# Wide attention of a fused decoder: the maxima turned and placed in halves of eight heads, exponentials 13 steps behind the maxima

## The chip, the cores and the metric

The kernel runs on one core of a Trainium2 chip. A core has five engines that this text speaks of: TensorE (PE, whose weight loads the profile lists as PEld), VectorE (DVE), ScalarE (ACT), GpSimd (POOL) and SyncE (SP), which here only issues DMAs. Each works through its own list of instructions in order and waits on semaphores for the others. The metric is the time of one execution on the device in microseconds; lower is better.

## The reference

Twelve residual steps over x of shape (4, 256, 128), four sequences ("batches" b = 0 to 3 below) of 256 tokens. The change lies in the stage that does three of them together: the quantised feedforward of the third layer, and the attention and the cross attention of the fourth.

```python
x = x + _L2_ffn_ref(_layernorm(x), ...)     # two 1.58-bit linear layers, 128 -> 512 -> 128, with layernorm, gelu
x = x + _L3_attn_ref(_layernorm(x), ...)    # the wide attention: 16 heads of 64
x = x + _L3_xattn_ref(_layernorm(x), ...)   # per token, 16 x 16 products of heads

def _L3_attn_ref(x, Wq, bq, Wk, bk, Wv, bv, Wo, bo):
    q, k, v = ...                                # (batch, 16 heads, 256, 64) each
    pattern = jnp.einsum('bhid,bhjd->bhij', k, q) / jnp.sqrt(64)
    prob = jax.nn.softmax(pattern, axis=-2)      # over the keys, for each query
    out = jnp.einsum('bhis,bhid->bhsd', prob, v)
    return concat(out) @ Wo + bo
```

## The kernel before, in words

The stage is `feedforward_attentions`. It is written as a row of steps, from -26 on. Every engine walks through the same steps in order; a semaphore, not a step, is what makes it wait. There are 64 units of the wide attention (4 batches of 16 heads). Step s does, among other things:

- PE `first(s)` (L2133, L2134): the scores of unit s, queries on the partitions, into one of two PSUM banks. The contraction is over 64 rows, and the head's parity decides which half of the array's rows it uses (`r = 64 * (h % 2)`).
- DVE `maxima(s)` (L2392): the largest score of each query. After the last head of a batch four small operations (L2398 to L2404) split the 32 columns of maxima into three bf16 parts.
- PE `second(s - WIDE_LAG)` (L2146, L2147): the scores again, keys on the partitions, minus the maxima, which come in as a product of ones with `MTR`. It also contracts over 64 rows, of the half that its own head's parity gives. ACT (L2249) takes the exponential.
- PE `weighted(s - WIDE_LAG - 1)` (L2163): probabilities times values, over all 128 rows, and every second step DVE `normalise` (L2410, L2412).

The maxima have to get from the partitions to the rows that `second` reads. That is the chain M: PE turns them (job "M", L2094), ACT copies them out (L2217), and SP's queue places them in `MTR` with six DMAs (L2492).

Beside the units runs a plan of jobs, each with a step of its own, at most two to a step (`place` takes the next free step when one is full). A job is some matmuls of PE into one of two banks and a copy out by ACT or DVE. Kinds: f1 to f4 the feedforward, T and xT transposes, q, k and v the projections of the wide attention (L2085, L2089), M the turned maxima, t and o its output projection, x... the cross attention. Pieces such as "gelu" or "products" are work of ACT, DVE and POOL at a given step; the cross attention of a batch is a chain of POOL products (L2456, L2467), DVE sums and an ACT exponential. PE's order inside a step is: jobs, `first`, `second`, `weighted`. ACT's is: copies of jobs, gelu (L2239), the exponential of the cross attention, then the exponential of the unit.

The rule of the plan for batch b before: M at step 16b+18, v from 16b+15, the output projection (t, o) from 16b+40. The feedforward of batch 2 begins at step 1, that of batch 3 at step 16. With `WIDE_LAG` 21, steps 0 to 20 have `first` without `second`, steps 21 to 63 have both, and steps 64 to 84 have `second` without `first`.

Of the kernel before, what the change touches and what calls it, by code (L numbers as in the profile page):

```python
# [9 lines left out]
BF16 = mybir.dt.bfloat16  # L10
I32 = mybir.dt.int32
ALU = mybir.AluOpType
ACT = mybir.ActivationFunctionType
AX_X = mybir.AxisListType.X
# [442 lines left out]
WIDE_LAG = 21  # L457
# [1464 lines left out]
def feedforward_attentions(c):  # L1922
# [9 lines left out]
    MX = s(2 * 32).rearrange("p (r c h) -> p r c h", r=2, c=2)  # L1932
    MR = s(32).rearrange("p (c h) -> p c h", c=2)
    MP = s(2 * 96, BF16).rearrange("p (r c m) -> p r c m", r=2, c=2)
    MT = s(256, BF16)[0:48, :]
# [48 lines left out]
    for b in range(B):  # L1984
        place(16 * b + 18, "M", b, 0)
        for i in range(6):
            place(16 * b + 40 + i + i // 3, ("t", "t", "o")[i % 3], b, i)
# [3 lines left out]
    for b in range(B):  # L1991
# [18 lines left out]
        for i in range(4):  # L2010
            place(16 * b + 15 + i, "v", b, i)
# [16 lines left out]
    assert all(job_at["k", b, i] <= 16 * b + 4 * i and job_at["v", b, 3] < 16 * b + 22 for b in range(B) for i in range(4))  # L2028
# [16 lines left out]
    def tensor(pe, own):  # L2045
# [3 lines left out]
        def run_job(i, kind, b, m):  # L2049
# [41 lines left out]
            elif kind == "M":  # L2091
                pe.wait_ge(max_parts, b + 1)
                for qc in range(2):
                    last = nc.tensor.transpose(out[0:48, 64 * qc:64 * qc + 64].bitcast(BF16), MP[:, b % 2, qc, :], c.identb)  # L2094
# [41 lines left out]
        def second(i):  # L2136
            b, h = i // HEADS, i % HEADS
            if h == 0:
                pe.wait_ge(max_placed, 16 * 6 * (b + 1))
# [27 lines left out]
        for step in range(FROM, TO):  # L2167
            for job in [(i,) + j[1:] for i, j in enumerate(jobs) if j[0] == step]:
                run_job(*job)
            if step == FROM + 8:  # L2170
                pe.wait_ge(fills, 3)
# [13 lines left out]
    def scalar(act, own):  # L2185
# [4 lines left out]
        act.wait_ge(fills, 3)  # L2190

        def leave(i, kind, b, m):
# [21 lines left out]
            elif kind == "M":  # L2214
                if b >= 1:
                    act.wait_ge(max_placed, 16 * 6 * b)
                ins = nc.scalar.copy(MT, out[0:48, 0:128].bitcast(BF16))  # L2217
# [33 lines left out]
    def vector(dve, own):  # L2251
# [137 lines left out]
        def maxima(a):  # L2389
            b, h = a // HEADS, (a % 2) * 8 + a % HEADS // 2  # L2390
            dve.wait_ge(qk1, a + 1)
            nc.vector.tensor_reduce(MX[:, b % 2, :, h], PS[:, a % 2, :].rearrange("p (c k) -> p c k", c=2), AX_X, ALU.max).then_inc(max_done, 1)  # L2392
            if a % HEADS == HEADS - 1:
                dve.wait_ge(max_done, a + 1)
                own.settle()
                m = MX[:, b % 2, :, :]
                part = [MP[:, b % 2, :, 16 * i:16 * i + 16] for i in range(3)]
# [20 lines left out]
        for step in range(FROM, TO):  # L2418
# [11 lines left out]
            if step == FROM + 9:  # L2430
                dve.wait_ge(bout_psum, 1)
                dve.wait_ge(fills, 3)
# [4 lines left out]
    def gpsimd(pool, own):  # L2437
# [37 lines left out]

        nc.gpsimd.memset(VB[:, :, :, :, WIDE:WIDE + 1], 1.0).then_inc(fills, 1)
# [9 lines left out]
    def sync(sp, own):  # L2486
        sp.wait_ge(fills, 3)
        for b in range(B):
            sp.wait_ge(*emptied("M", b, 0))
            for part in range(3):  # L2490
                for r in range(2):
# [324 lines left out]
```

## Time and profile before

| | |
|---|---|
| median of 3 runs | 1174.65 us (1174.62 to 1174.73) |
| the profiled execution's own time | 1175.91 us |
| span of its profile | 1174.1 us |
| PE, DVE, ACT, POOL busy | 73%, 51%, 30%, 29% of the span |
| mean clock granted to PE | 0.834 of full |

The span is the time from the first to the last instruction of one profiled execution; the time of that execution is 1.8 us longer. Step 0 of the stage's units begins at 709.8 us, and the following layer's feedforward fills the span from about 1040 us on. The granted clock is 1 at 2.4 GHz and 0.5 at 1.2 GHz.

### The profile page before, as it was taken

What the parts mean: (1) busy time and instruction counts of PE and PEld (TensorE: products, weight loads), DVE (VectorE), ACT (ScalarE), POOL (GpSimd) and SP (SyncE); (2) the same over time, 40 slices, a digit from 0 to 9 for tenths busy, and PEclk for the clock granted to TensorE, in tenths of its full rate; (3) what the DMA queues carried; (4) which work ended last, traced back from release to release, by engine and by line L of the source; (5) the groups of instructions that cost most, each with busy time, mean ns of one, the idle gap of its engine ahead of it and who ended that gap; (6) DMA issues with size and microseconds to landing.
All of it is one profiled execution on the core that took longest, in us unless ns stands there. A gap on an engine that the chain in (4) does not pass through costs nothing. (4 is left out here: it accounts for less than half of the span.)

```text
span 1174.1 us, 15927 instructions
## 1 busy us (share of the span) xinstructions
PE 854.0 (73%) x5969; PEld 617.9 (53%) x5969; DVE 596.9 (51%) x1400; ACT 352.5 (30%) x685; POOL 339.9 (29%) x324
## 2 busy tenths in 40 slices
PE   5964887945664465798879327999999997157994
PEld 2541454633442453576645215567878776134994
DVE  2655843214599814775654466755336444342222
ACT  1110674220122012165446212344343332011331
POOL 1363101223088422222310210000034347625131
PEclk9985997975697677799889657789999998558897
DMA  9202200640000025063560000000000000004584
GB/s 391 92 1 80 68 4 1 181 116 1 19 0 1 1 44 127 22 133 77 132 175 4 1 1 0 1 1 2 1 2 1 3 1 1 0 1 169 190 274 151
DMA packets 44677, 72.43 MB, mean 62 GB/s; under 512 B 4817, under 2 KB 36737, under 8 KB 43033
## 3 DMA queue, kind: packets, MB, share of 16 engines
q1 hardware_dynamic: 38921, 65.72, 18.9%
q0 software_dynamic: 1728, 3.59, 0.9%
q10 hardware_dynamic: 3952, 2.10, 0.7%
q8 instruction: 48, 0.79, 0.3%
q14 instruction: 28, 0.23, 0.1%
HBM read 58.65 MB, written 15.89 MB: 63 GB/s over the span
## 5 line engine op out<-in xcount | busy, mean ns | idle before, releaser
L842 DVE TENSOR_REDUCE space<-PS 128x2 f32<-128x512 f32 x128 | 83.5, 687 | 41.7 <-PE PS L651 41.3
L2392 DVE TENSOR_REDUCE space<-PS 128x2 f32<-128x512 f32 x64 | 44.0, 688 | 91.9 <-PE PS L2134 91.7
L826 ACT ACTIVATE annex<-PS 128x384 f32<-128x384 f32 (+1 forms) x128 | 66.9, 545 | 54.1 <-PE PS L660 24.3
L2146 PE MATMUL PS<-space 64*128 64x256 f32 x256 | 80.9, 409 | 0.0
L2163 PEld LDWEIGHTS PS<-space 128*128 128x128 f32 x512 | 63.5, 195 | 20.9 <-issue 20.0
L2163 PE MATMUL PS<-space 128*128 128x65 f32 x512 | 72.3, 286 | 0.2 <-ACT space L2249 0.2
L1913 POOL TENSOR_TENSOR space<-space 128x1536 f32<-128x1536 f32 x16 | 54.6, 3441 | 37.7 <-ACT space L1786 31.4
L1133 PE MATMUL PS<-space 128*128 128x128 f32 x444 | 57.3, 284 | 8.6 <-DVE space L1268 2.6
L2249 ACT ACTIVATE space<-PS 128x512 f32<-128x512 f32 x64 | 38.2, 597 | 75.6 <-PE PS L2147 75.5
L1133 PEld LDWEIGHTS PS<-space 128*128 128x128 f32 x444 | 53.6, 197 | 11.3 <-issue 6.1
L1268 DVE TENSOR_TENSOR space<-PS,space 128x512 f32<-128x512 f32 (+1 forms) x28 | 19.2, 687 | 72.3 <-ACT space L1195 67.1
L2133 PE MATMUL PS<-space 64*128 64x256 f32 x128 | 45.1, 463 | 1.6 <-issue 1.0
L2441 POOL TENSOR_SCALAR var_eps<-moments 128x2 f32<-128x2 f32 x16 | 3.5, 222 | 140.5 <-DVE moments L2258 140.5
L2467 POOL TENSOR_TENSOR weights<-const_tile,annex 128x2048 f32<-128x2048 f32 x8 | 43.3, 5442 | 3.0 <-ACT const_tile L2243 3.0
L2456 POOL TENSOR_TENSOR weights<-CTX,annex 128x2048 f32<-128x2048 f32 x8 | 35.8, 4490 | 26.3 <-ACT CTX L2230 26.3
L2146 PEld LDWEIGHTS PS<-space 64*128 64x128 f32 x256 | 38.6, 189 | 5.7 <-issue 1.8
L226 PE MATMUL PS<-small_tile 128*128 128x512 bf16 x40 | 17.6, 620 | 30.5 <-DVE moments L211 29.8
L826 ACT ACTIVATE space<-PS 128x512 f32<-128x512 f32 x64 | 35.7, 599 | 11.6 <-PE PS L662 10.6
L2085 PE MATMUL PS<-XT,weights 128*128 128x256 f32 x128 | 38.4, 444 | 0.6 <-ACT XT L2200 0.6
L1303 POOL DMA_INDIRECT l_ffn_y<-space x22 | 21.1, 960 | 60.7 <-ACT space L1186 60.7
L2134 PE MATMUL PS<-space 64*128 64x256 f32 x128 | 38.6, 408 | 0.0
L2147 PE MATMUL PS<-space,small_tile 64*128 64x256 bf16 x128 | 35.0, 273 | 0.0
(488 smaller groups left out, 2241.1 us busy)
## 6 DMA issues: line engine op xcount, KB each, us to landing
space<-in_e_l_ffn SPq DMA_DIRECT2D x22, 768.0 KB
space<-in_e_l_ffn SPq DMA_DIRECT2D x23, 192.0 KB, 2.7
l_ffn_sorted<-in_slots SPq DMA_DIRECT2D x2, 1584.0 KB, 25.5
space<-l_attn_scratch_k SPq DMA_DIRECT2D x8, 384.0 KB
space<-l_ffn_sorted SPq DMA_DIRECT2D x10, 264.0 KB, 5.1
weights<-in_w_l_xattn SPq DMA_DIRECT2D x1, 2504.0 KB, 15.3
weights<-in_w_l_attn SPq DMA_DIRECT2D x1, 2124.0 KB, 12.0
space<-l_xattn_scratch_q SPq DMA_DIRECT2D x4, 512.0 KB, 3.5
```

The costliest lines, as they stand in the source:

```text
L826: nc.scalar.activation(P[:, u % 8, 0:keys], PS[:, 3 + u % 2, 0:keys], ACT.Exp).then_inc(exp_done, 1)
L842: nc.vector.tensor_reduce(m[:, :, at_h], PS[:, u % 3, :].rearrange("p (c k) -> p c k", c=2), AX_X, ALU.max).then_inc(max_done, 1)
L1133: last = nc.tensor.matmul(PS[:, 2 * kind + g % 2, 128 * i:128 * i + 128], weight(b, kind, chunk), x, start=True, stop=True)
L1913: nc.gpsimd.tensor_tensor(PR[:, j - 1, :, :], Q[:, t % 2, :, :], bcast(KG[:, t, j, :], 1, 16), ALU.mult).then_inc(prod, 1)
L2085: last = nc.tensor.matmul(out[:, 256 * (g % 2):256 * (g % 2) + 256], w[:, 128 * g:128 * g + 128], c.XT[:, sl], start=True, stop=True)
L2133: nc.tensor.matmul(PS[:, a % 2, 0:256], q[:, 0:128], kk, start=True, stop=True)
L2134: nc.tensor.matmul(PS[:, a % 2, 256:512], q[:, 128:256], kk, start=True, stop=True).then_inc(qk1, 1)
L2146: nc.tensor.matmul(out, kk[:, 128 * kc:128 * kc + 128], q, start=True, stop=False)
L2163: last = nc.tensor.matmul(out, p[:, 256 * kc + 128 * qc:256 * kc + 128 * qc + 128], VB[:, b % 2, kc, h, :], start=kc == 0, stop=kc == 1)
L2249: nc.scalar.activation(P[:, i % 3, :], PS[:, 3 + i % 2, :], ACT.Exp).then_inc(exp_done, 1)
L2392: nc.vector.tensor_reduce(MX[:, b % 2, :, h], PS[:, a % 2, :].rearrange("p (c k) -> p c k", c=2), AX_X, ALU.max).then_inc(max_done, 1)
L2467: nc.gpsimd.tensor_tensor(PR[:, t, :].rearrange("p (h d g) -> p h d g", h=16, d=8), bcast(e[:, t, :].rearrange("p (h g) -> p h g", h=16), ...
```

## The change

Heads are treated in halves of eight. The split of the maxima, the job M and the six DMAs run once per half, so twice as often, each on half as many columns or rows (`out[0:32]` in place of `out[0:48]`, four partitions read per DMA instead of eight). `second` waits at every eighth head for the half's placement. The plan changes with it: M at 16b+10 and 16b+18, v from 16b+8, t and o from 16b+32, and everything that follows o eight steps earlier. `WIDE_LAG` is 13. As the split now fills 24 of 32 columns, `MP` is cleared once, by one more memset. `maxima` numbers heads so that each half of eight has its own block.

```diff
-WIDE_LAG = 21
+WIDE_LAG = 13
...
     MTR = s(2 * 8 * 256, BF16).rearrange("p (r g t) -> p r g t", r=2, g=8)
-    MX = s(2 * 32).rearrange("p (r c h) -> p r c h", r=2, c=2)
-    MR = s(32).rearrange("p (c h) -> p c h", c=2)
-    MP = s(2 * 96, BF16).rearrange("p (r c m) -> p r c m", r=2, c=2)
-    MT = s(256, BF16)[0:48, :]
+    MX = s(2 * 16).rearrange("p (r c h) -> p r c h", r=2, c=2)
+    MR = s(16).rearrange("p (c h) -> p c h", c=2)
+    MP = s(2 * 64, BF16).rearrange("p (r c m) -> p r c m", r=2, c=2)
+    MT = s(256, BF16)[0:32, :]
...
     for b in range(B):
-        place(16 * b + 18, "M", b, 0)
+        for half in range(2):
+            place(16 * b + 8 * half + 10, "M", b, half)
         for i in range(6):
-            place(16 * b + 40 + i + i // 3, ("t", "t", "o")[i % 3], b, i)
+            place(16 * b + 32 + i + i // 3, ("t", "t", "o")[i % 3], b, i)
...
         for i in range(4):
-            place(16 * b + 15 + i, "v", b, i)
+            place(16 * b + 8 + i, "v", b, i)
...
     assert all(x[0] < y[0] for x, y in zip(jobs, jobs[2:]))
-    assert all(job_at["k", b, i] <= 16 * b + 4 * i and job_at["v", b, 3] < 16 * b + 22 for b in range(B) for i in range(4))
+    assert all(job_at["k", b, i] <= 16 * b + 4 * i and job_at["v", b, 3] < 16 * b + 14 for b in range(B) for i in range(4))
...
             elif kind == "M":
-                pe.wait_ge(max_parts, b + 1)
+                pe.wait_ge(max_parts, 2 * b + m + 1)
                 for qc in range(2):
-                    last = nc.tensor.transpose(out[0:48, 64 * qc:64 * qc + 64].bitcast(BF16), MP[:, b % 2, qc, :], c.identb)
+                    last = nc.tensor.transpose(out[0:32, 64 * qc:64 * qc + 64].bitcast(BF16), MP[:, m, qc, :], c.identb)
...
             b, h = i // HEADS, i % HEADS
-            if h == 0:
-                pe.wait_ge(max_placed, 16 * 6 * (b + 1))
+            if h % 8 == 0:
+                pe.wait_ge(max_placed, 16 * 6 * (i // 8 + 1))
...
             elif kind == "M":
-                if b >= 1:
-                    act.wait_ge(max_placed, 16 * 6 * b)
-                ins = nc.scalar.copy(MT, out[0:48, 0:128].bitcast(BF16))
+                if 2 * b + m >= 1:
+                    act.wait_ge(max_placed, 16 * 6 * (2 * b + m))
+                ins = nc.scalar.copy(MT, out[0:32, 0:128].bitcast(BF16))
...
         def maxima(a):
-            b, h = a // HEADS, (a % 2) * 8 + a % HEADS // 2
+            half, h = a // 8, (a % 2) * 4 + a % 8 // 2
             dve.wait_ge(qk1, a + 1)
-            nc.vector.tensor_reduce(MX[:, b % 2, :, h], PS[:, a % 2, :].rearrange("p (c k) -> p c k", c=2), AX_X, ALU.max).then_inc(max_done, 1)
-            if a % HEADS == HEADS - 1:
+            nc.vector.tensor_reduce(MX[:, half % 2, :, h], PS[:, a % 2, :].rearrange("p (c k) -> p c k", c=2), AX_X, ALU.max).then_inc(max_done, 1)
+            if a % 8 == 7:
...
                 own.settle()
-                m = MX[:, b % 2, :, :]
-                part = [MP[:, b % 2, :, 16 * i:16 * i + 16] for i in range(3)]
+                m = MX[:, half % 2, :, :]
+                part = [MP[:, half % 2, :, 8 * i:8 * i + 8] for i in range(3)]
...
 
+        nc.gpsimd.memset(MP, 0.0).then_inc(fills, 1)
...
     def sync(sp, own):
-        sp.wait_ge(fills, 3)
+        sp.wait_ge(fills, 4)
         for b in range(B):
-            sp.wait_ge(*emptied("M", b, 0))
-            for part in range(3):
-                for r in range(2):
-                    sp.dma_start(MTR[64 * r + part:64 * r + part + 1, b % 2, :, :],
-                                 MT[16 * part + 8 * r:16 * part + 8 * r + 8, :]).then_inc(max_placed, 16)
+            for half in range(2):
+                sp.wait_ge(*emptied("M", b, half))
+                for part in range(3):
+                    for r in range(2):
+                        sp.dma_start(MTR[64 * r + part:64 * r + part + 1, b % 2, 4 * half:4 * half + 4, :],
+                                     MT[8 * part + 4 * r:8 * part + 4 * r + 4, :]).then_inc(max_placed, 16)
```

How instructions move on PE, at the first steps with the new lag. The rows are PE's list, where L2134 and L2135 are `first`, L2147 and L2148 `second`, L2164 `weighted`, L2086 the jobs q and k (all one line further down in the changed file). Of the kernel before, steps 13 to 15:

```order
L2085 MATMUL PS<-XT,weights 128x256 x4
L2133 MATMUL PS<-space 128x256
L2134 MATMUL PS<-space 128x256
L2133 MATMUL PS<-space 128x256
L2134 MATMUL PS<-space 128x256
L2085 MATMUL PS<-XT,weights 128x256 x2
L2089 MATMUL PS<-weights,XT 128x512
L2133 MATMUL PS<-space 128x256
L2134 MATMUL PS<-space 128x256
L2085 MATMUL PS<-XT,weights 128x256 x2
```

Of the change, steps 13 and 14:

```order
L2086 MATMUL PS<-XT,weights 128x256 x4
L2134 MATMUL PS<-space 128x256
L2135 MATMUL PS<-space 128x256
L2147 MATMUL PS<-space 128x256
L2148 MATMUL PS<-space,small_tile 128x256
L2147 MATMUL PS<-space 128x256
L2148 MATMUL PS<-space,small_tile 128x256
L2134 MATMUL PS<-space 128x256
L2135 MATMUL PS<-space 128x256
L2147 MATMUL PS<-space 128x256
L2148 MATMUL PS<-space,small_tile 128x256
```

`second` now follows `first` from step 13 on, and the v job (L2089) is gone from between them. It has moved, with the M job, to steps 8 to 11, where PE's list of the change reads as follows (L2090 is v, L2095 M, L2080 the transpose T of batch 1, L2064 the feedforward's f2):

```order
L2090 MATMUL PS<-weights,XT 128x512
L2134 MATMUL PS<-space 128x256
L2135 MATMUL PS<-space 128x256
L2095 MATMUL PS<-small_tile,space 32x128 x2
L2090 MATMUL PS<-weights,XT 128x512
L2134 MATMUL PS<-space 128x256
L2135 MATMUL PS<-space 128x256
L2080 MATMUL PS<-const_tile,XN 128x128 x2
L2090 MATMUL PS<-weights,XT 128x512
L2134 MATMUL PS<-space 128x256
L2135 MATMUL PS<-space 128x256
L2064 MATMUL PS<-weights,const_tile 128x512 x2
```

Before, the list had there:

```order
L2133 MATMUL PS<-space 128x256
L2134 MATMUL PS<-space 128x256
L2133 MATMUL PS<-space 128x256
L2134 MATMUL PS<-space 128x256
L2063 MATMUL PS<-weights,const_tile 128x512 x2
L2133 MATMUL PS<-space 128x256
L2134 MATMUL PS<-space 128x256
L2079 MATMUL PS<-const_tile,XN 128x128 x2
L2133 MATMUL PS<-space 128x256
L2134 MATMUL PS<-space 128x256
L2133 MATMUL PS<-space 128x256
L2134 MATMUL PS<-space 128x256
```

What moved: one v or M job now stands ahead of each `first` of steps 8 to 11, and f2 (with the gelu behind it) slipped from step 10 to step 12. On ACT the gelu of batch 2 and the first exponential of a unit now share step 13:

```order
L2208 ACTIVATE space<-PS,space 128x256 x2
L2240 ACTIVATE weights<-weights 128x512 x2
L2250 ACT_TABLE_LOAD
L2250 ACTIVATE space<-PS 128x512 x2
L2210 ACTIVATE space<-PS,weights 128x256 x2
```

where before the first exponentials stood behind copies alone:

```order
L2198 COPY const_tile<-PS 128x1024
L2209 ACTIVATE space<-PS,weights 128x256 x2
L2249 ACT_TABLE_LOAD
L2249 ACTIVATE space<-PS 128x512 x2
```

The stage has three table loads from its first exponential on in both: one ahead of that exponential, and two around the gelu of batch 3.

## Rows read from the trace of the kernel before

**Rows 1.** Stretches of the stage: us, busy time by engine, PEclk, DMA

```profile
732.50:746.50 14.00, 11.24 (x34) 6.80 (x34) 7.27 (x17) 2.63 (x6) 0.94 (x2) 0.52 0.01 1
746.50:764.50 18.00, 17.80 (x75) 10.85 (x74) 15.87 (x38) 9.47 (x20) 2.30 (x6) 1.00 0.01 1
764.50:777.70 13.20, 11.96 (x96) 9.02 (x94) 10.21 (x29) 4.68 (x8) 1.45 (x3) 1.00 0.00 1
777.70:790.70 13.00, 11.60 (x46) 8.84 (x46) 3.15 (x8) 6.12 (x9) 0.00 (x0) 0.61 0.00 0
790.70:915.40 124.70, 124.12 (x884) 96.74 (x883) 60.62 (x136) 48.62 (x94) 24.93 (x14) 1.00 0.01 2
915.40:971.00 55.60, 55.60 (x351) 42.77 (x351) 21.03 (x45) 18.79 (x35) 24.64 (x13) 1.00 0.01 2
```

**Rows 2.** The chain that ended last, from 971 us: start, us, what

```profile
971.08 8.96 POOL weights L2456 x2
```

**Rows 3.** Timeline, a step with `first` and `second`, and the next step

```profile
819.10 0.48 PE L2133 MATMUL PS<-space 64*128 64x256 f32 x1
819.11 0.48 PE L2146 MATMUL PS<-space 64*128 64x256 f32 x1
...
821.43 0.48 PE L2133 MATMUL PS<-space 64*128 64x256 f32 x1
```

**Rows 4.** Timeline, steps 70 to 71, `second` without `first`

```profile
933.67 0.70 PE L2146 MATMUL PS<-space 64*128 64x256 f32 x2
...
935.99 0.70 PE L2146 MATMUL PS<-space 64*128 64x256 f32 x2
```

**Rows 5.** Timeline of PE, steps 11 to 18 in part

```profile
740.81 0.66 PE L2079 MATMUL PS<-const_tile,XN 128*128 128x128 f32 x2 [2.70 <-DVE XN L2263]
...
746.54 0.71 PE L2133 MATMUL PS<-space 64*128 64x256 f32 x4
...
747.61 1.13 PE L2085 MATMUL PS<-XT,weights 128*128 128x256 f32 x4
...
752.51 0.70 PE L2133 MATMUL PS<-space 64*128 64x256 f32 x2
...
753.57 1.13 PE L2085 MATMUL PS<-XT,weights 128*128 128x256 f32 x4
754.53 1.02 PE L2089 MATMUL PS<-weights,XT 128*128 128x512 f32 x2
755.48 0.70 PE L2133 MATMUL PS<-space 64*128 64x256 f32 x2
...
756.54 0.29 PE L2094 MATMUL PS<-small_tile,space 128*48 128x128 bf16 x2
756.76 1.13 PE L2089 MATMUL PS<-weights,XT 128*128 128x512 f32 x2
```

**Rows 6.** Timeline of ACT around gelu 3, with PE just ahead

```profile
779.10 0.41 PE L2079 MATMUL PS<-const_tile,XN 128*128 128x128 f32 x2 [1.43 <-DVE XN L2263]
...
779.94 1.28 ACT L2239 ACT_TABLE_LOAD   x1
781.23 1.15 ACT L2239 ACTIVATE weights<-weights 128x512 f32<-128x512 f32 x2
782.40 1.28 ACT L2249 ACT_TABLE_LOAD   x1
783.70 0.60 ACT L2249 ACTIVATE space<-PS 128x512 f32<-128x512 f32 x1
```

**Rows 7.** Timeline of SP, the six placing DMAs of batch 0

```profile
757.33 4.22 SPq L2492 DMA_DIRECT2D space<-space  x6
```

**Rows 8.** DMA issues, another SBUF-side store: KB, us to landing

```profile
l_attn_scratch_q<-space SPq DMA_DIRECT2D x10, 128.0 KB, 1.9
```

**Rows 9.** Timeline, matmuls with one output partition (tile 128*1), what follows

```profile
675.33 3.07 PEld L2173 LDWEIGHTS PS<-weights 128*1 128x1 f32 x16 [0.19 <-issue]
678.83 0.13 PEld L2063 LDWEIGHTS PS<-weights,const_tile 128*128 128x128 bf16 x2 [0.43 <-issue]
```

More of the change, by code:

```diff
@@ L2170, in tensor @@
             if step == FROM + 8:
-                pe.wait_ge(fills, 3)
+                pe.wait_ge(fills, 4)
                 for ch in range(8):
@@ L2189, in scalar @@
         act.wait_ge(bias_ready, 1)
-        act.wait_ge(fills, 3)
+        act.wait_ge(fills, 4)
         def leave(i, kind, b, m):
@@ L2431, in vector @@
                 dve.wait_ge(bout_psum, 1)
-                dve.wait_ge(fills, 3)
+                dve.wait_ge(fills, 4)
                 nc.vector.tensor_tensor(bout[0:1, :], PS[0:1, 6, 0:128], WA["bo"], ALU.add).then_inc(bout_ready, 1)
```

## The prediction

> **What bounds the kernel now.** I read the stretches first [rows 1]. From 790.7 to 971.0 us PE is busy 179.7 of 180.3 us at granted clock 1.00, while DVE has 81.7: the stage goes at PE's pace from about step 29 of the units on. From 746.5 to 764.5, steps 13 to 20, PE is busy 17.8 of 18.0, so it sets the pace there too, with DVE (15.9) close behind. Ahead of that, from 732.5 to 746.5, PE is busy 11.2 of 14.0 at a mean clock of 0.52 and waits on DVE, the longest wait being 2.70 us for the normalised tile that T turns [rows 5]. From 777.7 to 790.7 the clock is 0.61. Then the chain that ended last [rows 2]: from 971.08 on it is the product of batch 2's cross attention on POOL, and after that a latency chain of cross attentions and the last feedforward. That product waits for a job of PE's three steps before the last `second`, both before and after the change, and the plan behind it keeps its distances. So the tail is as long as before, and the change is worth what it takes off PE between step 8 and job xq of batch 2.
>
> **What the lag is worth.** `first` and `second` contract over 64 rows each, and with an odd lag their heads differ in parity, so they use different halves of the array. The trace shows what comes of it: at 819.10 and 819.11 both start together, and the step lasts 821.43 - 819.10 = 2.33 us [rows 3]. A step with `second` alone lasts 935.99 - 933.67 = 2.32 us [rows 4]. So a `first` beside a `second` is free, and the 21 steps without a partner at the end gain nothing from being alone. A `first` alone, between two jobs, costs 753.57 - 752.51 = 1.06 us; two in a row, of opposite parity, cost 747.61 - 746.54 = 1.07 together [rows 5]. With lag 13 (odd too) the `first` of steps 13 to 20 get partners: one pair of 1.07 and six singles of 1.06, the last some 0.1 cheaper because its neighbour already shared its mode. **Gain 7.3 us.** The Trainium skill (TensorEngine Tiling (Array Packing), Key Properties) says that tiles work independently, and the starts 0.01 us apart agree.
>
> **Jobs that move ahead.** The four v jobs of batch 0 and its M leave steps 15 to 18. A v job takes 755.48 - 754.53 = 0.95 us and M 756.76 - 756.54 = 0.22 [rows 5], 4.0 us in all, at full clock. They go to steps 8 to 11, into the stretch from 732.5 on. There PE then has, at full clock, five lone `first` (5.3; the jobs break up today's pairs), four v and M (4.0), two jobs q and k at 0.96 (1.9) and about 1.0 of f1, f2 and T: 12.2 us, against 14.0 us that pass today with half of this work. Today 0.96 of that time is at the low clock (mean 0.52), 13.4 us; in the other stretch of low clock, where PE had work all along, it is 0.39 x 2 x 13.0 = 10.1 us [rows 1]. With 10.1 us low, 5.05 of work is done in them and 7.15 behind them: 17.25 us, 3.25 later than now. **Net gain 4.0 - 3.25 = 0.7 us.** Its ends: no low clock, 12.2 us, a gain of 5.8; low throughout, 24.4 us, a loss of 6.4; low for today's 13.4 us, a loss of 0.9. I take the middle, since PE will hardly wait there: the wait of 2.70 is covered by v jobs.
>
> **Twice as many M.** From step 13 to batch 2's xq there are seven instead of three. At 0.22 each the four more cost 0.9. The transposes now have 32 output columns and not 48. The Trainium skill (same page, Key Properties) says that a change of tiling mode drains TensorE; were 32 columns a mode of their own, each M would bring two changes. The rows bound this: around the matmuls with a tile of 128*1 PE's loads wait 0.19 before and 0.43 after [rows 9], 0.62 a job at half clock, times eight is 5.0 on top, 5.9 in all; the 48 columns of today show nothing behind them (M ends as v begins). I take 2.0, nearer to today's form. **Loss 2.0.** By the row of today's M alone it would be 0.9. The four more splits on DVE and 24 more DMAs on SP's queue lie beside PE: DVE has 98.6 us free in 790.7 to 971.0, SP nothing else queued here, and for batch 0 the split stands behind the maximum of step 7, three steps ahead of its M. Without that cover a split of four operations would put under 1 us into the chain per half.
>
> **The first exponential.** ACT's step 13 now holds the copies of k and q, gelu (1.15), a table load (1.28) and the exponential (0.60) [rows 6]. The k copy ends about 1.0 us after the `first` of step 13 begins, so the exponential is out at 1.0 + 1.15 + 1.28 + 0.60 plus hand-over, 4.2. PE does two pairs of 1.3 and would want it at 2.9. `weighted(0)` waits 1.3, once; `second(2)` and all of PE's later work queue behind it. **Loss 1.3.** Today nothing waits there. The Trainium skill (ScalarE: Activation LUTs, What ACT_TABLE_LOAD costs) gives 1283 ns for a load and 1380 ns of drain besides. The load agrees at 1.28; the drain is not seen, as the exponential starts at 783.70 where its load ends at 783.68 [rows 6]. With a drain the loss would be 2.7 and the forecast 1.4 us higher. At the second spot, the gelu of batch 3, PE waits 1.43 for T today [rows 6]; in the change T stands two steps ahead of that gelu with a v job beside it, and is ready. Today the low clock makes PE slow enough for the late exponential (load, gelu, load, exponential) not to be waited for, and I leave the low clock there. **Gain 1.4.** In steps 17 to 20 DVE has as much to do as PE (15.9 of 18.0 today), so job f3, behind the quantisation, may wait: **loss 0.5**, between 0 and 1.5.
>
> **The placement.** From M to the landing it takes 757.33 + 4.22 - 756.54 = 5.0 us to the last issue [rows 5, 7] and 1.9 to land, by the nearest store [rows 8]: 6.9. `second` comes three steps behind M as it did, and the shortest such stretch (M at 18, `second` at 21) holds three steps of 2.33, M, two jobs q and k and f3: 9.5 us. No wait.
>
> **Sum.** 7.3 + 0.7 - 2.0 - 1.3 + 1.4 - 0.5 = 5.6 us. The profiled execution took 1175.91 (span 1174.1 and 1.8 around it) and would take 1170.3; it is 1.3 above the median, so the median goes from 1174.65 to 1169.1.
>
> **The rivals.**
> - The low clock of the stretch from 777.7 does not come back. The 13.0 us there hold T (0.3), two steps of 2.33 and two jobs (1.9), 6.9 at full clock. At full clock PE does wait for the exponential: 1.0 for the k copy, 1.28 + 1.15 + 1.28 + 0.60 and hand-over 0.1 are 5.4, wanted at 2.33 + 1.3 + 0.3 = 3.9, so 1.5. The term is then 13.0 - 6.9 - 1.5 = 4.6 in place of 1.4. For it: T's wait just ahead goes away, and PE has more to do in steps 13 to 28. Against: waits of 1.3 and 1.5 us remain, and today's fall came behind one of 1.43. Time 1165.9; if the jobs of steps 8 to 11 run at full clock too, 1160.8. Chance 0.23.
> - Low clock elsewhere, or M in a mode of its own. The wait of `weighted(0)` starts one more stretch with 10.1 us at half rate (5.05): 1174.2; or the M cost 5.9 instead of 2.0: 1173.0. Both reach back to no change. Chance 0.2.
> - It doesn't do what it says: DVE sets the pace of steps 13 to 20, so that partners for `first` gain nothing. Then 7.3 falls away: 1176.4. Against: PE's 17.8 of 18.0 there. Chance 0.03.
> - Slower: the clock stays low from step 8 until past the wait of `weighted(0)`. Steps 8 to 12 then take 24.4 us (term -6.4 instead of 0.7), and two pairs and a `weighted` (3.7) take as much again: 1169.1 + 7.1 + 3.7 = 1179.9. Slower by over 0.2% it is once low clock costs 8.0 more than I count, 16 us of it. For it: the clock is 0.52 there now. Against: today's low stretches end while PE works. Chance 0.06.
> - Slower: placement late. It starts beyond 9.5 us and must cost 1.0 in each of eight halves (5.6 + 2.35), so a landing 3.6 us later than by the nearest store; at 4.5 later, 8 x 1.9 = 15.2 are lost, 1184.3. Against: today's `second` never waits on it. Chance 0.03.
>
> **How the numbers follow.** My forecast, with its smaller terms at their ends 1167 to 1172, has 0.45. A measurement of this kernel tells about 0.2%, 2.35 us, from no change. Faster by more (below 1172.3) are the forecast and the first rival, and 0.02 of the second: 0.45 + 0.23 + 0.02 = 0.70. The same are the rest of the second and the third with 0.02: 0.20. Slower are both last rivals and 0.01 of the third: 0.10. The range goes from 1163.5 (the first rival with half of its second step) to 1175.5 (the second with both of its parts in good measure); outside are the far ends of the first and the slower cases, some 0.17.
>
> **What the changed profile would show.** `first` and `second` starting together from step 13 on; the chain's POOL product starting about 5.6 us earlier than 971.08; the same 203 us from there to the end; M at about 0.2 to 0.8 us; a wait of 1 to 1.5 us on ACT ahead of `weighted(0)`; the stretch of steps 8 to 12 some 3 us longer, with a clock of about 0.6 to 0.7. I would be wrong if the mean clock from step 8 to 31 differed much from today's, if L2095 brought gaps of PE around it, or if `second` waited for the DMAs.

## The result and the profile after

| | before | after |
|---|---|---|
| median | 1174.63 us (4 runs, 1168.86 to 1174.73) | 1186.58 us (4 runs, 1183.01 to 1191.04) |
| ratio, 95% interval | | 1.0125 [1.0089, 1.0160] |
| span of the profile | 1174.1 us | 1181.0 us |
| mean clock granted to PE | 0.834 | 0.837 |

The change makes the kernel slower by 1.25%; the forecast was faster by 0.5%. A ratio is an estimate of its own, from fast executions alone, and not the quotient of the medians (1.0102 here; below the two differ by up to 0.005). Line numbers are one higher now (`first` L2134 and L2135, `second` L2147 and L2148, `weighted` L2164, v L2090, q and k L2086, M L2095). The stretches of the profile after, with the columns of [rows 1]:

```profile
732.00:758.70 26.70, 23.02 (x42) 10.94 (x42) 6.66 (x16) 3.91 (x8) 0.93 (x2) 0.50 0.00 1
758.70:800.00 41.30, 38.20 (x274) 29.04 (x273) 28.39 (x79) 18.62 (x35) 3.73 (x8) 0.99 0.01 1
800.00:860.00 60.00, 55.63 (x400) 43.45 (x400) 28.31 (x69) 26.03 (x49) 1.87 (x4) 1.00 0.01 2
860.00:875.00 15.00, 11.56 (x72) 7.70 (x71) 10.36 (x13) 4.65 (x9) 9.85 (x4) 1.00 0.01 2
875.00:892.00 17.00, 16.75 (x74) 12.64 (x74) 6.03 (x11) 3.84 (x8) 0.02 (x1) 0.60 0.00 0
```

The columns are the stretch, its length, the busy time (and number of instructions) of PE, PEld, DVE, ACT and POOL, the granted clock, and the DMA's share and rate. Two places stand out against [rows 1]. The work of steps 8 to 12 lasts 26.7 us at clock 0.50, where 14.0 us at 0.52 were enough before. And from 860 to 875 PE, which had no wait over 0.26 us there before, is busy for only 11.56 of 15.0 us, and behind that the clock is low once more. PE's timeline at the first place and on to `weighted(0)`:

```profile
732.86 2.08 PE L2090 MATMUL PS<-weights,XT 128*128 128x512 f32 x2 [2.18 <-DVE X L2379]
...
740.87 0.39 PE L2095 MATMUL PS<-small_tile,space 128*32 128x128 bf16 x2
741.19 2.08 PE L2090 MATMUL PS<-weights,XT 128*128 128x512 f32 x2
...
746.66 0.66 PE L2080 MATMUL PS<-const_tile,XN 128*128 128x128 f32 x2 [1.39 <-DVE XN L2264]
...
755.44 3.78 PE L2086 MATMUL PS<-XT,weights 128*128 128x256 f32 x8 [1.44 <-DVE weights L2372]
759.15 0.65 PE L2134 MATMUL PS<-space 64*128 64x256 f32 x1
759.16 0.65 PE L2147 MATMUL PS<-space 64*128 64x256 f32 x1
...
763.18 1.08 PE L2164 MATMUL PS<-space 128*128 128x65 f32 x8 [1.31 <-ACT space L2250]
```

A v job takes 2.08 us, twice the 1.02 of [rows 5]: all four run at the low clock, which lasts from 732.2 to 759.5. The first of them waits 2.18 us for a bank that DVE empties. From step 13 on `first` and `second` start together, and `weighted(0)` waits 1.31 us for the exponential, both as predicted. At the second place, all engines:

```profile
866.08 8.94 POOL L2457 TENSOR_TENSOR weights<-CTX,annex 128x2048 f32<-128x2048 f32 x2 [4.10 <-issue]
...
867.79 7.31 DVE L2264 TENSOR_SCALAR XN<-X,moments,rstd 128x128 f32<-128x128 f32 x2
...
875.02 0.68 DVE L2393 TENSOR_REDUCE space<-PS 128x2 f32<-128x512 f32 x1
875.25 0.41 PE L2080 MATMUL PS<-const_tile,XN 128*128 128x128 f32 x2 [3.28 <-DVE XN L2264]
875.59 0.79 PE L2134 MATMUL PS<-space 64*128 64x256 f32 x1
```

DVE's two normalising operations of batch 3 take 7.31 us together, 2.88 and 4.51; their median before is 0.341 each. Each ends within 0.1 us of one of POOL's two products of batch 0 (866.08 + 8.94 = 875.02). PE waits 3.28 us for the rows, and its next `first` starts at 0.79 instead of 0.48: the clock has fallen, and stays low to 889.2. The chain that ended last is entered later than in [rows 2]:

```profile
984.58 8.96 POOL weights L2457 x2
```

That is 984.58 - 971.08 = 13.5 us later, not 5.6 earlier. From there to the end of the span it takes 196.4 us, not 203.0. Nothing of the change lies there; executions differ in it, so the medians and not the spans are compared.

### The profile page after: what moved, and what is told of

Same layout as the page of the kernel before. It is cut to its first block and busy times, and to the rows that moved or that the text cites. A ratio compares the mean times of both kernels' runs of the same rounds, so it can differ in the third digit from the quotient of the medians.

```text
span 1181.0 us, 16003 instructions
## 1 busy us (share of the span) xinstructions
PE 850.0 (72%) x5977; PEld 612.7 (52%) x5977; DVE 606.2 (51%) x1416; ACT 352.9 (30%) x689; POOL 339.5 (29%) x325
## 5 line engine op out<-in xcount | busy, mean ns | idle before, releaser
L2147 PE MATMUL PS<-space 64*128 64x256 f32 x256 | 82.2, 414 | 0.0
L2164 PEld LDWEIGHTS PS<-space 128*128 128x128 f32 x512 | 63.5, 195 | 23.8 <-issue 23.8
L2164 PE MATMUL PS<-space 128*128 128x65 f32 x512 | 72.2, 285 | 3.1 <-ACT space L2250 3.1
L2134 PE MATMUL PS<-space 64*128 64x256 f32 x128 | 48.2, 464 | 1.6 <-issue 1.0
L2135 PE MATMUL PS<-space 64*128 64x256 f32 x128 | 41.3, 410 | 0.0
L2147 PEld LDWEIGHTS PS<-space 64*128 64x128 f32 x256 | 39.4, 193 | 3.3 <-issue 0.8
L2086 PE MATMUL PS<-XT,weights 128*128 128x256 f32 x128 | 38.6, 449 | 2.0 <-DVE weights L2372 1.4
L1303 POOL DMA_INDIRECT l_ffn_y<-space x22 | 21.1, 957 | 55.8 <-ACT space L1186 55.8
L2148 PE MATMUL PS<-space,small_tile 64*128 64x256 bf16 x128 | 35.2, 275 | 0.0
```

What stands on the lines that cost most here:

```text
L2086: last = nc.tensor.matmul(out[:, 256 * (g % 2):256 * (g % 2) + 256], w[:, 128 * g:128 * g + 128], c.XT[:, sl], start=True, stop=True)
L2134: nc.tensor.matmul(PS[:, a % 2, 0:256], q[:, 0:128], kk, start=True, stop=True)
L2135: nc.tensor.matmul(PS[:, a % 2, 256:512], q[:, 128:256], kk, start=True, stop=True).then_inc(qk1, 1)
L2147: nc.tensor.matmul(out, kk[:, 128 * kc:128 * kc + 128], q, start=True, stop=False)
L2164: last = nc.tensor.matmul(out, p[:, 256 * kc + 128 * qc:256 * kc + 128 * qc + 128], VB[:, b % 2, kc, h, :], start=kc == 0, stop=kc == 1)
```

## The experiments

For each kernel I read two lengths from its trace, by the starts of DVE's `maxima`: from step 8 to step 13, and from step 13 to POOL's product of batch 2. The second holds what lies behind the moved v jobs of batch 0. Together they divide a result between the two places, but for one part: the v job of step 8 stands ahead of that step's maximum. From the maximum of step 7 to that of step 8 it is 6.87 us in the change and 2.71 before, so where a v job is at step 8 the first length is some 4 us short of the loss. When an edit moves a job, `place` can shift its neighbours by a step or more; where that matters it is said. Edits that bring v later also widen the assertion on its steps, which is not shown.

| kernel | median us (runs) | ratio to the kernel before | steps 8 to 13 | step 13 to product |
|---|---|---|---|---|
| before | 1174.63 (4) | | 12.7 | 223.4 |
| the change | 1186.58 (4) | 1.0125 [1.0089, 1.0160] | 23.5 | 224.1 |
| e1_halves_only | 1175.77 (7) | 1.0042 [1.0012, 1.0071] | 12.1 | 231.3 |
| e2_cross0_later | 1201.38 (4) | 1.0247 [1.0210, 1.0283] | 23.6 | 239.0 |
| e3_v_in_twos | 1165.01 (10) | 0.9962 [0.9933, 0.9992] | 21.1 | 213.6 |
| e4_lag22 | 1213.15 (4) | 1.0355 [1.0321, 1.0390] | 12.7 | 267.2 |
| e5_norm_earlier | 1176.58 (11) | 1.0066 [1.0032, 1.0100] | 24.1 | 215.2 |
| e6_before_v_early | 1206.83 (5) | 1.0357 [1.0312, 1.0401] | 20.9 | 246.6 |
| e7_v0_by_need | 1153.32 (5) | 0.9872 [0.9833, 0.9912] | 11.9 | 212.2 |
| e8_lag15 | 1171.32 (11) | 1.0003 [0.9973, 1.0033] | 14.8 | 225.3 |
| e9_norm_on_product | 1167.60 (12) | 0.9965 [0.9931, 0.9999] | 12.5 | 224.3 |
| e10_before_v_as_e7 | 1194.65 (6) | 1.0222 [1.0169, 1.0274] | 11.9 | 243.3 |
| e11_only_v0_later | 1168.59 (12) | 0.9992 [0.9960, 1.0024] | 11.9 | 224.1 |
| e12_v0_later_norm_earlier | 1164.34 (12) | 0.9949 [0.9917, 0.9981] | 12.5 | 217.4 |

The kernel before, run beside them, had medians of 1168.67 (e1 to e4), 1170.35 (e5 to e8), 1171.11 (e9, e10) and 1170.75 (e11, e12), single runs between 1162.7 and 1183.5. Microseconds below that come from two ratios are their difference times 1171.

**e1_halves_only.** The change with the old distance: only the halves are left.

```diff
-WIDE_LAG = 13
+WIDE_LAG = 21
-            place(16 * b + 32 + i + i // 3, ("t", "t", "o")[i % 3], b, i)
+            place(16 * b + 40 + i + i // 3, ("t", "t", "o")[i % 3], b, i)
-            place(16 * b + 8 + i, "v", b, i)
+            place(16 * b + 15 + i, "v", b, i)
```

> Only the halves: maxima split, turned and placed in halves of eight, with the lag of 21 and the jobs v, t and o where the kernel before has them. If the eight smaller M jobs are what costs (theory M: each brings gaps of PE, up to 0.62 us on top of 0.22, as in the prediction's rival), this takes 1177 to 1181. If the changed plan and lag are what cost (theory plan: low clock in steps 8 to 12, and batch 3's normalisation held up on DVE beside batch 0's POOL product), this takes 1174 to 1177 and the L2095 rows show no gap behind them.

It came out 0.42% above, 4.9 us: its 1175.77 us lie in the range of theory plan, but the kernel before had come down to 1168.67 beside it, so the number does not choose. The rows of L2095 show no gap behind them but where PE waits for DVE. The second length is 7.9 us longer than before, and 6.9 of that lie ahead of step 30: from step 30 on to the product it is 173.8 us against 172.8. So twice as many M cost PE about 1 us from there on. Ahead of it the job f3 of step 20 waits for the quantisation on DVE. That stands behind the additional split, and a step later than before (18 and not 17), as M at step 10 pushed an f2 and the gelu back by one:

```profile
761.09 0.61 PE L2070 MATMUL PS<-small_tile,weights 128*128 128x128 bf16 x8 [2.30 <-DVE weights L2287]
```

2.30 us where it waited 0.20 before, and a low stretch of 10.2 us more follows from 769.8.

**e2_cross0_later.** The change with the whole cross attention of batch 0 five steps later.

```diff
-    first_x = [job_at["o", b, 5] + 1 for b in range(B)]
+    first_x = [job_at["o", b, 5] + 1 + (5 if b == 0 else 0) for b in range(B)]
```

> The changed kernel with the cross attention of batch 0 five steps later, so that its POOL products start at step 48 and not beside DVE's normalisation of batch 3 (step 42). Theory lock: in the changed kernel's trace that normalisation (L2264) takes 7.3 us for two and ends with the POOL product, PE waits 3.3 us for it and then has 13.7 us at the low clock; without the overlap both go, 9 to 10 us: 1173 to 1178, and no L2264 over 0.6 us before 900 us. Rival (the wait there is DVE's own backlog or PE pace, and the time is lost elsewhere): 1183 or more, with the wait of PE on L2264 still there.

1201.38 us, far from theory lock and in the range of the rival. The product of batch 0 leaves the normalisation alone, and meets the split of the maxima instead (DVE's and POOL's timeline):

```profile
886.13 8.97 POOL L2457 TENSOR_TENSOR weights<-CTX,annex 128x2048 f32<-128x2048 f32 x2 [8.14 <-ACT space L2208]
887.41 3.26 DVE L2399 TENSOR_SCALAR space<-space 128x16 bf16<-128x16 f32 x1
890.71 4.43 DVE L2401 SCALAR_TENSOR_TENSOR space<-space 128x16 f32<-128x16 f32 x1
...
913.09 10.85 POOL L2468 TENSOR_TENSOR weights<-const_tile,annex 128x2048 f32<-128x2048 f32 x2 [0.74 <-ACT const_tile L2244]
918.62 5.36 DVE L2401 SCALAR_TENSOR_TENSOR space<-space 128x16 f32<-128x16 f32 x1
```

Operations on 16 columns whose like take 0.17 to 0.19 us elsewhere take 3 to 5 us, and end when one of POOL's does: 886.13 + 8.97 is 895.10, and 890.71 + 4.43 is 895.14. M and the placement of a half are behind them. The collision follows POOL's products; which operation of DVE it meets depends on the plan.

The rest of the loss has a further cause. PE waits twice more for rows that DVE normalises, 5.30 us at 929.05 and

```profile
957.11 0.66 PE L2111 MATMUL PS<-const_tile,CTX 128*128 128x128 f32 x2 [8.33 <-DVE CTX L2264]
```

and DVE's operation was not held there. It started 8.12 us late, because it needs a small result that POOL computes, and in POOL's own order that stood behind the products of batch 1 (946.44 to 955.34). Low stretches of 13.7, 13.7 and 6.8 us begin at 925.5, 952.8 and 973.3. So the shift of five steps made new collisions, and the run does not price the old one.

**e3_v_in_twos.** The change with v in pairs at 16b+9 and 16b+12. The planner then moves neighbours too: the normalisation of batch 3 is at step 41, no longer 42, with the product still at 43.

```diff
-            place(16 * b + 8 + i, "v", b, i)
+            place(16 * b + 9 + 3 * (i // 2), "v", b, i)
```

> The changed kernel with the v jobs in twos (steps 16b+9 and 16b+12) in place of one each at 16b+8 to 16b+11. f2 of batch 2 is back at steps 10 and 11, its gelu at step 12, and batch 3's normalisation a step earlier (41, products at 43). Theory clock: in the traces so far the granted clock rises only in or just behind an unbroken run of 3 us or more of 128-row fp32 matmuls (the q and k jobs); two v jobs in a row give such a run at step 9, so the low stretch that began at 732 ends at about 740 to 743 and not at 759.5, step 13 begins 8 to 10 us earlier, and the time is 1170 to 1176 (with the normalisation ahead of the product). Rival (the low clock in steps 8 to 12 comes from waits, 2.2 and 1.4 us, not from what PE does): low until step 13 again, 1178 or more.

By the ratios 19 us below the change, more than was forecast, and not for the reason given: the first length is still 21.1, where step 13 was to begin 8 to 10 us earlier. The second length falls by 10.5 to 213.6: there is no long operation on DVE. The clock comes back inside the second pair of v and not the first:

```profile
734.54 3.78 PE L2090 MATMUL PS<-weights,XT 128*128 128x512 f32 x4 [1.13 <-DVE X L2379]
...
748.25 3.30 PE L2090 MATMUL PS<-weights,XT 128*128 128x512 f32 x4
751.48 0.70 PE L2134 MATMUL PS<-space 64*128 64x256 f32 x2
```

**e4_lag22.** The kernel before with `WIDE_LAG = 22`, so that `first` and `second` of a step have the same parity and use the same rows of the array.

```diff
-WIDE_LAG = 21
+WIDE_LAG = 22
```

> The kernel before with a lag of 22 in place of 21, so that first and second of a step have heads of the same parity and use the same half of the array. Theory pairs (the prediction's step of 7.3 us): a first beside a second is free only because it uses the other half; with 42 steps of both in the same half each costs 0.7 to 1.06 more, 29 to 45 us: 1204 to 1220. Rival (it is free because PE has slack in the step): within 5 us of 1174.6.

3.55% slower, as the theory had it. The second length grows by 43.8 us over the 42 steps that have both, of which one low stretch from 768.5 (34.1 us, so up to 17 lost) is a part. So a `first` that has to share its rows with `second` costs 0.6 to 1.05 us a step.

**e5_norm_earlier.** The change with only the normalisation of batch 3 one step ahead.

```diff
-        piece(f + 3, "normed", b)
+        piece(f + (2 if b == 3 else 3), "normed", b)
```

> The changed kernel with one piece moved: the normalisation of batch 3 (DVE, before job T of batch 3) at step 41 in place of 42, so that it is over when POOL's product of batch 0 begins. Theory lock: DVE's normalisation and POOL's product can't run at the same time; two instructions of 0.34 us took 2.9 and 4.5 us and ended with the products. Moved, they take 0.34 each, the wait of PE (3.3 us) and the 13.7 us of low clock behind it go: 9 to 10 us less than the changed kernel (ratio to it 0.992), step 43 of the units at about 865 and not 875. In the run with the cross attention later the same happened to the split of the maxima instead (3.3 and 4.4, then 5.4 us). Rival (the normalisation was slow for another reason): no change in its length and the same time as the changed kernel.

The two operations take at most 0.34 us each, the second length falls from 224.1 to 215.2, and the ratio from 1.0125 to 1.0066 (6.9 us, give or take 6; 9 to 10 were expected). The first length stays at 24.1. No other job moves in this edit.

**e6_before_v_early.** The kernel before, where only the v jobs go to 16b+8 to 16b+11.

```diff
-            place(16 * b + 15 + i, "v", b, i)
+            place(16 * b + 8 + i, "v", b, i)
```

> The kernel before, lag 21 and whole batches, with only the v jobs at 16b+8 to 16b+11 in place of 16b+15 to 16b+18. Theory clock: a v job ahead of each lone first of steps 8 to 11 at half rate keeps PE at the low clock until the q and k jobs of step 13; steps 8 to 13 take 20 to 24 us and not 12.7, later steps give back 4: 4 to 8 us slower than the kernel before. Rival (in the changed kernel the stretch is long because of M and the later f2, or by the phase in which the clock is looked at): steps 8 to 13 within 17 us, time within 2 us of the kernel before.

Without halves and without the shorter distance the first length is 20.9, so the v jobs suffice: the clock is low from 732.8 to 756.7 but for 3.4 us. The larger loss was expected by nobody. In the steps of `second` alone, from which the v jobs of batch 3 were taken, PE works 47.8 us at the low clock; e10 below shows the same. And f3 of batch 2 waits 6.28 us for the quantisation, which slipped from step 17 to 19 in this plan while f3 went from 20 to 21.

**e7_v0_by_need.** e3's plan, with batch 0's v out of the steps 8 to 12.

```diff
-            place(16 * b + 9 + 3 * (i // 2), "v", b, i)
+            place(16 * b + ((14, 19, 14, 21) if b == 0 else (9, 9, 12, 12))[i], "v", b, i)
```

> The kernel with v in twos, with the v jobs of batch 0 where they are first needed: two at step 14, one at 19 and one at 21, so steps 8 to 12 hold only what they hold before, and M. Theory clock: steps 8 to 13 back to 13 to 15 us (21.1 with v in twos), 3.9 given back later, 2 to 4 us faster than v in twos, 0.6 to 0.9% faster than the kernel before. Rival (low clock comes anyway, from the waits for DVE): as v in twos, within 2 us.

The best kernel of the study: 1.28% faster than the one before, where 0.6 to 0.9% was forecast. Steps 8 to 13 take 11.9 us, and from 741.7 to 967 us the clock is never low (windows and timeline of PE):

```profile
743.90:771.80 27.90, 27.55 (x180) 19.80 (x178) 19.61 (x49) 14.44 (x27) 2.81 (x6) 1.00 0.00 1
771.80:801.80 30.00, 29.83 (x204) 21.69 (x202) 14.43 (x42) 15.57 (x28) 0.94 (x2) 1.00 0.01 2
```

**e8_lag15.** The change with a distance of 15, M at 16b+12 and 16b+20, t and o from 16b+34, v two to a step at 16b+14 and 16b+15.

```diff
-WIDE_LAG = 13
+WIDE_LAG = 15
-            place(16 * b + 8 * half + 10, "M", b, half)
+            place(16 * b + 8 * half + 12, "M", b, half)
-            place(16 * b + 32 + i + i // 3, ("t", "t", "o")[i % 3], b, i)
+            place(16 * b + 34 + i + i // 3, ("t", "t", "o")[i % 3], b, i)
-            place(16 * b + 8 + i, "v", b, i)
+            place(16 * b + 14 + i // 2, "v", b, i)
```

> Halves with a lag of 15: M at 16b+12 and 16b+20, v at 16b+14 and 16b+15, t and o from 16b+34. Six first instead of eight get a partner at the start (5.6 us by the pairs' price, not 7.3), and steps 8 to 13 are as before but for M at 12. The normalisation of batch 3 is at step 42, the product of batch 0 at 45: no overlap. By theories lock and clock together it is 4 to 8 us faster than the kernel before. If the gain of the pairs is not there to be had (rival), it is equal to it or slower.

The same as the kernel before, where 4 to 8 us less were expected. The first length is 14.8 and no operation is held up, but a low stretch of 17.1 us stands at 786.8, and two more `first` are without a partner.

**e9_norm_on_product.** The collision, put into the best kernel.

```diff
-        piece(f + 3, "normed", b)
+        piece(f + (4 if b == 3 else 3), "normed", b)
```

> The kernel with batch 0's v at steps 14, 19, 14 and 21, with one thing more: DVE's normalisation of batch 3 a step later, at step 42, where it meets GpSimd's product of batch 0 (step 43), as it does in the changed kernel. Theory 'the two engines hold one another off': one or two of DVE's normalising operations take 3 to 5 us where the median is 0.34, PE waits some 3 us for the normalised rows, and the stage gets 3 to 10 us longer (the upper end with a low stretch of the clock behind it): 1157 to 1164 us. Rival 'the collision costs nothing by itself, the changed kernel was slow there by its clock alone': no operation over 1 us, or a long one without a wait, and 1153 us within 0.3%.

```profile
849.31 8.90 POOL L2457 TENSOR_TENSOR weights<-CTX,annex 128x2048 f32<-128x2048 f32 x2 [4.74 <-issue]
...
851.01 7.28 DVE L2264 TENSOR_SCALAR XN<-X,moments,rstd 128x128 f32<-128x128 f32 x2
...
858.44 0.66 PE L2080 MATMUL PS<-const_tile,XN 128*128 128x128 f32 x2 [7.35 <-DVE XN L2264]
```

The timeline of all engines shows the same 7.3 us, PE waits 7.35 us, and 13.7 us of low clock begin at 854.4. The ratio against e7 rises by 0.0093, 11 us: more than I gave. The wait of PE is longer than in the change, since T stands one step behind the normalisation here (43 and 42) and two steps in the change (44 and 42). Two operations of 0.34 us would have left about 0.6 of it, as PE had come to T at 851.09 and DVE began at 851.01.

**e10_before_v_as_e7.** The kernel before with e7's places for v.

```diff
-            place(16 * b + 15 + i, "v", b, i)
+            place(16 * b + ((14, 19, 14, 21) if b == 0 else (9, 9, 12, 12))[i], "v", b, i)
```

> The kernel before (full turns, 21 steps) with only the v jobs at the places of the best kernel so far: steps 14, 19, 14 and 21 for batch 0, 16b+9, 9, 12 and 12 for the others. Theory 'the pairs pay': the lone first of steps 13 to 20 and the lone second of the end stay alone, so the time stays by the kernel before, 1166 to 1174 us, 13 to 20 us above the kernel with both. Rival 'the v places alone pay': 1153 to 1160 us, and the shorter distance between maxima and exponentials is worth nothing. Third: v of the later batches at early steps draws DVE and the clock into a new low stretch as all four early v did: over 1180 us.

2.2% slower, which is the third case: v's places are no gain by themselves. Behind the last `first` (windows and timeline of PE):

```profile
910.60:918.00 7.40, 6.33 (x41) 4.88 (x40) 4.35 (x20) 2.55 (x6) 2.48 (x5) 0.98 0.00 1
918.00:962.00 44.00, 44.00 (x152) 33.05 (x152) 8.53 (x14) 7.49 (x14) 15.14 (x4) 0.50 0.01 1
```

```profile
915.73 0.41 PE L2079 MATMUL PS<-const_tile,XN 128*128 128x128 f32 x2 [1.07 <-DVE XN L2263]
...
959.72 3.13 PE L2105 MATMUL PS<-weights,annex 128*128 128x128 f32 x16
```

The clock falls behind one wait of 1.07 us and stays low through 44.00 us in which PE is busy for 44.00: 22 us are lost. L2079 is here the transpose ahead of batch 1's cross attention. In the kernel before, v jobs stand in that place, the transpose does not wait, and the clock stays at 1.00 [rows 1].

**e11_only_v0_later and e12_v0_later_norm_earlier.** The change with batch 0's v at e7's places, and the same with e5's edit too.

```diff
-            place(16 * b + 8 + i, "v", b, i)
+            place(16 * b + ((14, 19, 14, 21)[i] if b == 0 else 8 + i), "v", b, i)
```

> The changed kernel with batch 0's v jobs at steps 14, 19, 14 and 21 in place of 8 to 11; the other batches' v and the normalisation of batch 3 stay (it still stands at step 42, next to GpSimd's product at 43). Theory 'two separate losses, the v jobs of steps 8 to 11 and the collision': steps 8 to 13 take some 12 us again instead of 23.5, the long normalising operations stay (2.9 and 4.5 us): about 1174 to 1178 us, 9 to 12 us below the changed kernel. Rival 'either cure alone does it all, since the clock's phase is what moves': 1165 us or less, and no long operation. Rival 'v0's place is worth nothing outside the kernel in which it was tried': 1184 us or more.

> The changed kernel with both edits: batch 0's v at steps 14, 19, 14 and 21, and the normalisation of batch 3 at step 41. Theory of two separate losses: each cure gives its 10 us beside the other, so 1164 to 1168 us, 18 to 22 us below the changed kernel and 3 to 6 below the kernel before; steps 8 to 13 in about 12 us, no normalising operation over 1 us. Rival 'the clock moves the loss elsewhere': no long operation and short steps 8 to 13, but new low stretches of 10 us or more between steps 13 and 63, and 1172 us or more.

| ratio to the kernel before | normalisation at 42, on the product | at 41, ahead of it |
|---|---|---|
| v of batch 0 at 8 to 11 | 1.0125 | 1.0066 |
| at 14, 19, 14, 21 | 0.9992 | 0.9949 |

The two cures add up: v by 0.0133 and 0.0117 (16 and 14 us), the normalisation by 0.0059 and 0.0043 (7 and 5 us), each give or take 0.005; the last is no more than its uncertainty. The v edit also brings f2 and the gelu of batch 2 a step or two earlier, which is not what helps: e3 has them there too, and its first length is 21.1. e11 still has the long operations (2.88 and 4.51 us) and e12 has none; e11 came out below its 1174 to 1178 us, e12 at the lower end of its range. With e9, the collision is worth 5 to 11 us. Rid of both, the change is 0.5% faster than the kernel before.

## Why the prediction was wrong

Two steps of it failed, each by about half of the miss: the term for steps 8 to 12, and the premise that all behind them keeps its distances. The start of step 13 against that of before (759.15 and 746.54) and the product of batch 2 split the miss of 5.6 + 13.5 = 19.1 us.

**Steps 8 to 12, the term +0.7: wrong by 9.4 us or more.** "With 10.1 us low, 5.05 of work is done in them" took a low stretch to have a length of its own, the same as elsewhere. It has none here. Step 13 starts 12.6 us later, not 3.25: all of the moved work ran at the low clock, to which my outer end (24.4 us) came near, and PE waited 2.18, 1.39 and 1.44 us where I had thought it would hardly wait. The change's profiled execution was 2.2 us ahead at the maximum of step 7, with all that moved still to come; from there on steps 8 to 12 are 14.9 us longer (30.3 against 15.4), and the term is off by 11.7. e11, which moves only the v jobs of batch 0 (and with them f2 and the gelu, above), takes it back (11.9 us), and e6 makes it in the kernel before; halves, M and distance are not needed for it. In both kernels the low stretch that began at 732 ended at the q and k jobs of step 13, within them at 745.9 before and 0.3 us behind them at 759.5 in the change: what was put ahead of these jobs ran low. The rival with the clock low from step 8, which I gave 0.06, is what happened as far as step 13. Its second part, low past `weighted(0)`, did not: the clock was up at 759.5.

**"The plan behind it keeps its distances": wrong by about 9 us.** It keeps them from o on, but the feedforward of batch 3 did not move along with the cross attention of batch 0, and this brought POOL's product of batch 0 from step 51 to 43, beside DVE's normalisation of batch 3 at 42. I counted work of DVE as hidden while DVE had free time; its free time was not what mattered. e5 took away the long operations and 8.9 us of the second length; e9 put the same 7.3 us into another kernel; e2 gave them to other operations. The Trainium skill (SBUF — State Buffer, Who interferes with whom) says that DVE and GpSimd arbitrate for one pair of ports as an exclusive lock, taken for a whole instruction; that `tensor_scalar` can contend for it in its two-port modes, and an operation with two inputs in SBUF does with a GpSimd one that reads SBUF; and that `tensor_reduce` does not. The traces agree: each long operation is a `tensor_scalar` or has two inputs in SBUF, and ends within 0.1 us of one of POOL's, while the maximum of step 42, a `tensor_reduce` at 866.63 us, 0.55 behind the start of the product, took its usual 0.69 us. No rival of mine had it.

**The rest behind step 13.** There the terms make 7.3 + 4.0 - 2.0 - 1.3 + 1.4 - 0.5 = 8.9 us, 4.0 of it the v jobs gone from there. To test them apart I split the second length into PE's work (its busy time, with time at the low clock counted half), what the low clock added, and the time in which PE was idle:

| step 13 to product, us | before | the change | e5 | e7 |
|---|---|---|---|---|
| length | 223.4 | 224.1 | 215.2 | 212.2 |
| work of PE | 214.9 | 204.9 | 205.1 | 208.5 |
| added by the low clock | 5.1 | 6.9 | 1.7 | 0.0 |
| PE idle | 3.4 | 12.3 | 8.4 | 3.7 |

The work fell by 10.0, where 7.3 + 4.0 - 2.0 = 9.3 was forecast: the price of the pairs was right, and e4 agrees with it. Two other things were not, and they nearly cancel. The low stretch of [rows 1] from 777.7, which the term +1.4 left where it was, did not come back in the change, whose clock is never low between 759.5 and 875.6. That is my first rival (0.23), worth 5.1 us less the wait on the exponential that it foresaw as 1.5 and that measured 1.77. And PE is idle for longer than the 0.4 us more that the terms add up to (1.3 + 0.5 - 1.4): without the collision's 3.3 it is 9.0 against 3.4. Of the small terms, M costs about 1 us and not 2.0 behind step 30, at 0.29 us a job (0.39 at the low clock) with no gap behind it; f3 waits 1.51, the far end of my range of 0 to 1.5; `weighted` waits 1.31 as forecast, and the 1.77 at the second spot; T's wait of 1.43 shrank to 0.67, but a v job waits 1.53 for its bank and a later transpose 1.18, for which I had no term. No `second` waited for its placement. That e12 comes out 0.5% faster, as was forecast for the change, is luck in this respect.

**What stays open.** Why the clock returns at one place and not another is read from rows only, below. Whether the v jobs keep it low by being there, or by the waits that come with them, was not separated. e1's 0.42% is put down to f3's wait and to a low stretch by one profile. e7's lead over e12 (0.77%) is accounted for in part: e7 has the other batches' v in pairs, no low stretch where e12 has two of 3.4 us, and no waits of 1.77 and 1.53 us, and is 5.2 us shorter in the second length.

## What to carry to other kernels

When one chain of a plan moves and another doesn't, list which pieces become neighbours, and look above all for DVE operations on SBUF beside long POOL operations: 0.34 us became 4.5 here with DVE half idle. Work put into the stretch of low clock cost double here (v jobs of 2.08 and not 1.02 us) and did not bring the clock back; price such work at the low clock throughout, or put it where the clock is up. And an engine that is always busy is no proof of full speed: read the granted clock of its stretches, ahead of and behind every gap of a microsecond.

## What was unexpected of the hardware

**Busy throughout, and still at the low clock.** The Trainium skill (TensorE: Matmul & The Clock Gate, Part 1) has sustained activity release the lower clock. These traces differ: in e10 it stayed at 0.50 through 44.00 us with PE busy for 44.00, in e6 through 48.00 of 48.00. The ends of matmuls are modelled in a profile, so this busy share is the profile's. Those stretches hold steps of `second` alone over 64 rows, `weighted` over 128 (1.97 us a step) and short jobs between.

As the clock rose, PE was often in an unbroken run of float32 matmuls over 128 rows and some 3 us long. It rose within such a run at 790.2 us in the kernel before,

```profile
787.47 3.32 PE L2085 MATMUL PS<-XT,weights 128*128 128x256 f32 x8
```

and so in e3 (748.25, 3.30 us), e4 (800.26, 3.10), e6 (975.19, 3.62), e7 (740.04, 2.80) and e10 (959.72, 3.13). It rose 0.3 us behind the end of one in the change (755.44, 3.78), and 1 to 2 us behind one at 889.2 in the change and 763.7 in e5. But this is a selection and no rule. It stayed low behind the first run of v jobs in e3 (734.54, 3.78 us), and in e10 through `weighted` and two jobs on 128 rows without a break from 924.15 to 927.93. It rose without such a run at 780.0 in e1 and 780.6 in e6, among steps of `first` and `second`; in e6 PE had waited 6.28 us until 775.92. What decides it was not tested.

**A lock is seen by ends, not by busy time.** The held operation is shown as busy from its own start, so DVE's busy share rises (10.36 of 15.0 us from 860) although it does nothing, and the wait appears at PE as one for DVE. Its duration against the median of the same line gives it away: 4.51 us against 0.341.
